# ScalarE's fp16 copy of each gated FFN row tile moves behind the next tile's tanh or conv read-out

## What is computed

```python
xn  = layernorm(x)
x   = x + (xn + mamba2(xn)) + ffn(xn)
# ffn: 512 -> 2048 -> 512
hidden = silu(xn @ W1.T) * (xn @ W3.T)
out    = fwht(hidden) @ W2.T
# mamba2: one projection to z (1024), xBC (1280), dt (16); a causal conv of 4 taps and silu on xBC;
# a state-space scan over chunks; y * silu(z); RMS norm; w_out (1024 -> 512)
```

## Time and profile before

| | |
|---|---|
| median of three runs | 968.58 us |
| the profiled execution | 965.39 us |
| its span, first to last instruction | 963.6 us |
| mean granted TensorE clock | 0.996 of full |
| busy: PE, DVE, ACT, POOL | 934.7 (97%), 555.8 (58%), 391.4 (41%), 276.1 (29%) us |
| chain that ended last, by engine | PE 67%, DVE 1%, DMA 1%, ACT 1% |
| ACT's copies, line 978 | 64, 40.2 us; before them ACT was idle for 141.3 us, waiting for DVE's line 1265 |
| POOL's `hid_lo`, line 1443 | 64, 71.2 us |

### The profile page before, as it was taken

How to read it: one execution, slowest core, us unless ns; L and a number is a source line. 1 busy time by engine, 2 the same in 40 slices (tenths; PEclk the granted TensorE clock), 3 DMA queues, 4 the chain that set the end, 5 groups by cost and what they waited for, 6 DMA issues and landing times.

```text
span 963.6 us, 13435 instructions
## 1 busy us (share of the span) xinstructions
PE 934.7 (97%) x5000; PEld 469.3 (49%) x5000; DVE 555.8 (58%) x955; ACT 391.4 (41%) x690; POOL 276.1 (29%) x354
## 2 busy tenths in 40 slices
PE   9899987989899999999999999999999999999998
PEld 4444443545344445555454445555445445555543
DVE  7876588875534756556532766566451666575421
ACT  6678874533323445233221434233222444343200
POOL 0000446352000116466110106565210104654410
PEclk9999999999999999999999999999999999999999
DMA  9798355434224335525223435436223435256123
GB/s 336 247 349 295 112 192 193 131 124 137 96 74 147 125 111 159 155 72 176 88 67 113 143 99 164 145 97 175 78 76 101 143 107 160 65 151 153 45 77 98
DMA packets 76208, 134.26 MB, mean 139 GB/s; under 512 B 7536, under 2 KB 20464, under 8 KB 74096
## 3 DMA queue, kind: packets, MB, share of 16 engines
q1 hardware_dynamic: 56640, 104.88, 34.1%
q10 hardware_dynamic: 19504, 28.53, 10.0%
HBM read 107.43 MB, written 25.95 MB: 138 GB/s over the span
## 4 chain that ended last, share of the span: by engine, by line
PE 67%; DVE 1%; DMA 1%; ACT 1%; issue 0%; DVEq 0%; ACTq 0%
PE ps L600 46%; PE ps L834 14%; PE ps L796 2%; PE ps L782 1%; PE ps L788 1%; PE ps L768 1%; DMA arena<-cs_rows 1%; PE ps L619 0%; PE ps L638 0%; PE ps L751 0%; PE ps L771 0%; DVE arena L1348 0%; DVE arena L1426 0%; ACT arena L1059 0%; DVE arena L1265 0%
## 5 line engine op out<-in xcount | busy, mean ns | idle before, releaser
L600 PE MATMUL ps<-xh,arena 128*128 128x512 f16 x1592 | 487.9, 379 | 3.4 <-DVE arena L1194 3.3
L600 PE MATMUL ps<-xl,arena 128*128 128x512 f16 x796 | 302.0, 379 | 0.0
L600 PEld LDWEIGHTS ps<-xh,arena 128*128 128x128 f16 x1592 | 158.3, 99 | 190.3 <-issue 5.9
L834 PE MATMUL ps<-arena 128*128 128x512 f16 x768 | 171.1, 379 | 0.0
L1443 POOL TENSOR_TENSOR arena<-arena 128x512 f16<-128x512 f32 x64 | 71.2, 1113 | 334.6 <-ACT arena L978 334.6
L1244 DVE SCALAR_TENSOR_TENSOR arena<-ps,cw,arena 128x511 f32<-128x511 f32 (+2 forms) x120 | 89.4, 747 | 66.9 <-ACT arena L968 65.0
L600 PEld LDWEIGHTS ps<-xl,arena 128*128 128x128 f16 x796 | 77.9, 98 | 88.7 <-issue 3.3
L834 PEld LDWEIGHTS ps<-arena 128*128 128x128 f16 x768 | 74.1, 98 | 91.2 <-issue 5.5
L978 ACT ACTIVATE arena<-arena 128x512 f16<-128x512 f32 x64 | 40.2, 629 | 141.3 <-DVE arena L1265 141.3
L1260 DVE SCALAR_TENSOR_TENSOR arena<-arena,ps 128x512 f32<-128x512 f32 x64 | 44.0, 687 | 77.3 <-ACT arena L973 77.0
L600 PE MATMUL ps<-wo_hi,arena 128*128 128x512 f16 x256 | 79.9, 384 | 3.6 <-DVE wo_lo L1333 3.4
(11 more groups left out here) (179 smaller groups left out, 1092.8 us busy)
## 6 DMA issues: line engine op xcount, KB each, us to landing
arena<-w_parts SPq DMA_DIRECT2D x198, 256.0 KB, 2.6
w_parts<-arena SPq DMA_DIRECT2D x66, 256.0 KB, 2.6
arena<-cs_rows ACTq DMA_DIRECT2D x16, 1024.0 KB, 5.7
arena<-w SPq DMA_DIRECT2D x24, 512.0 KB, 4.9
arena<-ecs_rows ACTq DMA_DIRECT2D x24, 256.0 KB, 6.9
arena<-x ACTq DMA_DIRECT2D x18, 256.0 KB, 3.4
w_mid<-arena SPq DMA_DIRECT2D x8, 512.0 KB, 3.5
arena<-w_mid SPq DMA_DIRECT2D x16, 256.0 KB, 2.6
```

Of the source, the lines that this page charges most:

```text
L600: ins = nc.tensor.matmul(out_ap, lhs(i, a), rhs(i, c), start=(i == 0 and s == 0), stop=(i == n - 1 and s == 2))
L834: ins = nc.tensor.matmul(bank(t), hw[a][:, i, t * P:(t + 1) * P], w2s[i % W2R][:, d, :], start=(i == 0 and s == 0), stop=(i == JF - 1 and ...
```

## The change

ACT's copy to `hid_hi` leaves the entry of its own U tile and is issued at the next projection tile of the stream, behind that tile's own ACT instruction: the tanh for an A or Z tile, the conv read-out (line 968) for a C tile. The 16th U tile of a batch has no next tile and keeps its copy in place. The wait that the copy needs (DVE's eviction of the U tile) and, for i = 0, the wait for the last G step of the batch before, go with it. Next tiles are A tiles but for two places in batches 1 to 3: C5 follows U0, and Z7 follows U1. No other engine's code changes. Since the list puts other entries between a U tile and the next tile, the copy now also stands behind ACT's part of those. 

```diff
+                def hidden_hi(key):
+                    i = key[1]
+                    if i == 0:
+                        act.wait_ge(w2_used.sem, w2_used.at(b, -1))
+                    act.wait_ge(evac.sem, evicted(b, key))
+                    nc.scalar.activation(hid_hi[:, i, :], hs[i % 2], ACT.Copy).then_inc(hid_h.sem, 1)
+
                 def finish(key):
...
                         nc.scalar.activation(slot, src, ACT.Tanh, scale=...).then_inc(tanh_ok.sem, 1)
-                    else:
-                        if i == 0:
-                            act.wait_ge(w2_used.sem, w2_used.at(b, -1))
-                        act.wait_ge(evac.sem, evicted(b, key))
-                        nc.scalar.activation(hid_hi[:, i, :], hs[i % 2], ACT.Copy).then_inc(hid_h.sem, 1)
+                    if p > 0 and STREAMS[b][p - 1][0] == "U":
+                        hidden_hi(STREAMS[b][p - 1])
                     if p > 0 and STREAMS[b][p - 1][0] == "C":
...
                         finish((kind, i))
+                        if POS[b][kind, i] == NT - 1:
+                            hidden_hi((kind, i))
```

## The result

The changed kernel takes 984.56 us in the median of 4 runs (984.15 to 985.51) beside 968.04 of the kernel before (4 runs, 964.78 to 969.43): a ratio of 1.0177 with the interval 1.0150 to 1.0204, slower by 16.5 us. The forecast was 974.2 with a range up to 980.0. The direction was right, the size was three times the +5.6 that I had worked out. The two profiled executions lie 20.1 us apart (985.51 and 965.39; spans 983.7 and 963.6), because the one of before was at the low end of its runs and the one of the changed kernel the highest of its four.

A forecast was written before the change was run, and what follows sets the result against it. PE bounds batches 1 to 3, with no idle time; in batch 0 PE also waits for late ACT and DVE. Batches 1 to 3 +6.6 and batch 0 -1 give +5.6 on 968.58: 974.2 us, range 967.5 to 980.0.

The forecast's parts named there:

- The slack of 1.6 us at S0: Batches 1 to 3: before the change, `Xdec` ended 1.6 us ahead of PE's start of S0.
- DVE first at the port: Batches 1 to 3, chunk 0: when `XD` ends, DVE's waiting mask product runs before `Xdec`, leaving PE idle 2.2 us at S0.
- The term was +6.6: Batches 1 to 3: PE idles 2.2 us ahead of S0 in each batch, 3 x 2.2 = +6.6 us.
- the size taken for the clock: Batches 1 to 3: PE's clock stays at 1.00 behind each S0 wait, adding nothing; bound 1.7 us more each.
- Other copies that move far ... I take 0: Copies of U5 and U9 move far, but POOL work behind them has 1 us or more slack: 0, bound +0.5 a batch.
- I let the ceiling of 13.2 go in full: Batch 0: four PE waits (9.8 us) and the clock behind two of them vanish entirely, -13.2 us.
- S0 was forecast with 5.5: Batch 0: S0 starts 4.4 to 6.6 us late behind U1's moved copy, taken as 5.5, plus 1.7 for the clock.
- S1 was forecast with 3: Batch 0: S1 starts about 3 us late behind U5's moved copy, plus 1.7 for the clock.
- One sign: Batch 0: waits at QS4 and W0 staying as before would mean a plain loss and a time above 980.
- POOL keeps its turn: Batches 1 to 3: `Xdec` runs right behind `XD` although DVE waits; +1.4 there, total 969.0 us; chance 0.10.
- Batch 0 pays for all: Batch 0 gains 9 us from the freed tanh, outweighing the +6.6 of later batches: 966.2 us; chance 0.10.
- The clock drops behind each S0: Batches 1 to 3: PE's clock falls behind each S0 wait, 3 x 1.7 = 5.1 us more: 979.3 us; chance 0.12.

The follow-up runs named there:

- pick_more: Kernel before with copies of U2, U3, U4 and U7 moved in batch 0, and all but U1's in batches 1 to 3: 960.70 us, ratio 0.9918.
- only_u11: Kernel before with only the copy of U11 of batch 0 moved: 970.56 us, ratio 1.0024.
- u11_home: Changed kernel, but the copy of U11 of batch 0 stays in its old place: 980.56 us, ratio 1.0131.
- b0_keep: Kernel before with copies moved in batch 0 only, all but those of U1, U5 and U11: 967.94 us, ratio 1.0005.
- keep9: Kernel before with copies moved in batch 0 only, all but those of U1, U5, U9 and U11: 962.76 us, ratio 0.9943.
- lo_first_late: Changed kernel, but in batch 0 DVE does an A tile's last weight split ahead of that tile's eviction: 981.94 us, ratio 1.0148.
- dec_first: Changed kernel, but in batches 1 to 3 POOL does `Xdec` of chunk 0 ahead of `XD`: 975.81 us, ratio 1.0075.
- pick: Kernel before with only the copies of U2, U3, U4 and U7 of batch 0 moved: 962.74 us, ratio 0.9948.
- later_only: Kernel before with copies moved in batches 1 to 3 only, batch 0 as before: 975.21 us, ratio 1.0083.

## Why the prediction was right in direction and wrong in size

**Batches 1 to 3: the mechanism right, the clock wrong.** The slack of 1.6 us at S0, DVE first at the port, no gain where PE has no gap, and 0 for the other copies: all stood (`Xdec` 3.95 us, PE 1.99 idle, pick_more). The term was +6.6 and the waits came to 6.0. What failed is the size taken for the clock, nothing for each wait. I gave 0.12 to a rival in which it falls behind S0, and argued against it from one stretch in which 2.0 us of idle had left it at 1.00. In the changed kernel it fell behind two of three such waits, and cost 1.4 and 1.7 more in them (3.6 and 3.9 against 2.2). This made 9.6 of 6.6.

**Batch 0, the step "Other copies that move far ... I take 0".** This is the step that failed worst: it took 0, with a bound of 0.5 a batch. I followed U5's and U9's copies by the distance they move and did not follow U11's, which passes ACT's part of E3, a place where ACT is idle for 9.86 us behind DVE. The rule that I had for S0 (what stands ahead of the copy's new place, and what stands behind `hid_lo` on POOL) was not applied to it. Of the 5.9 us of added wait at N2 it carries 3.6, and the clock behind the wait comes on top; only_u11 shows 3.1 us for it alone, u11_home 4.0 in the change. U9's, which I had followed and priced at 0, is worth 5.2 us between b0_keep and keep9. If the two add up, which no run shows, 9.2 us of batch 0 were lost at a term of 0.

**Batch 0, the contention.** In batches 1 to 3 I priced the meeting with DVE's mask product. In batch 0 I had "two short weight splits" of DVE in the sum for S0 as time that POOL waits, but not the other side: that a split itself can become twice as long (1.60 us for 0.75), all through the batch. DVE's 13.2 us more (133.24 to 146.44) lie mostly there. Y1 waits 4.0 instead of 2.1. That this comes from the splits is likely and not shown apart: it falls to 0.84 in lo_first_late, where they are shorter, but PE waits 2.0 at S1 ahead of it there. So the step "I let the ceiling of 13.2 go in full" failed too: of its 9.8 us of waits 7.1 went (1.3, 3.4 and 2.4 of 3.0), but Y1 rose by 1.9, and the clock fell at new places instead of the two old ones, as told below.

**Batch 0, S0 and S1.** S0 was forecast with 5.5 and measured 4.3. S1 was forecast with 3 and measured 0.5. The chain of my sum was nearly right, 7.0 us from the tanh of A6 (140.21) to S1 (147.23) instead of 7.6. But I took PE's step at its old distance of 4.9 from that tanh, and PE was ready only after about 6.5: behind waits of 0.6 at line 739 and 1.3 at line 810 the granted clock was 0.55 from 140 to 142 us and 0.60 from 142 to 144, where it was 1.00 before, and the matmuls ahead of S1 took 1.7 us longer.

**Batch 0, the clock.** I gave it 1.7 for each of S0 and S1 and took back 3.4 for two waits, so zero in all. Measured is 6.1 us of busy time, more than the added idle of 4.4. Behind each of the three long waits the matmuls are stretched: S0's to 3.75 us from 1.96, Y1's to 3.68 from 1.97 in the kernel before, and behind N2 the clock is at 0.53. That ahead of S1 is the fourth place.

The account: +10.5 instead of -1, and +9.6 instead of +6.6, makes 20.1 instead of 5.6 between the profiled executions. Two slips of the working do not change this: with batch 0 at +4 the sum is 979.2 and not the 978 given as the upper end of the forecast's own range, and the plain sum of POOL's instructions makes S0 3.5 us late, 4.4 only with one split of DVE. One sign did not separate what it should: the time came out above 980 although the waits at WOS and W0 were gone and QS4 had 0.6 left.

**The rivals.** "POOL keeps its turn" fell (3.95 us in all three batches, dec_first). "Batch 0 pays for all" fell for this change, but its mechanism is true of a part of it: pick gains 4.8 us. "The clock drops behind each S0" was half true. What is open is why it fell behind some waits of 1.99 us and not behind others: behind the same three waits it fell twice in the changed kernel, twice in later_only, once in u11_home and twice in lo_first_late (batches 2 and 3, 2 and 3, 2, and 1 and 3); and in pick_more it stayed at 1.00 behind waits of 2.1 to 2.3 us. No run separates the causes. Also not separated is how the rest of the loss in batch 0 divides between U9's copy and the others that start a leapfrog.

The sharing itself is as the Trainium skill has it ("SBUF — State Buffer", section "Who interferes with whom": a VectorE instruction with two SBUF inputs contends with a GpSimd instruction that reads SBUF, and the one issued first holds the shared ports for its whole instruction). This case agrees: the split of 106.06 ends at 107.66, so its own 0.75 began at 106.91, 0.2 ahead of the recorded end of `hid_lo`, and it stood still for 0.85 us because `hid_lo` had led by 0.03.

## What to carry to other kernels

When an instruction is moved in one engine's queue, write down for every single copy of it what blocking wait it now stands behind, and what stands behind its consumer on the next engine; the one that passes a wait on another engine is the dear one, and it need not be the one that moves past the most work. A move can also change which instructions of two engines start together, and make both longer without adding any: look for pairs released by the same producer. And move it per instance: here 46 moved copies gain 0.8%, by the four of batch 0 among them as far as the traces show, and 60 lose 1.8%.

## What was not expected of the hardware

- A start 0.03 us later costs an instruction nearly what the other one lasts (0.85 us beside 1.09), and it spreads: from 106.03 us on, POOL's three and DVE's three instructions take 1.09, 2.34, 2.34 and 1.60, 1.78, 3.98 us, where alone they take 1.09, 1.90, 1.90 and 0.75, 0.75, 2.29.
- In the two kinds of meeting looked at, when the holder ends and the other engine waits, the other goes next even if the holder's engine has its next instruction ready (`XD` and then the mask product at 373.58; `Xdec` at 109.38 ahead of the mask product issued at 109.89). Both cases fit "who waits longest"; for the second place the forecast had left the order open.
- The same idle of 1.99 us left the clock at 1.00 in one batch and was followed by 0.50 in two others.
- More idle can go with less time: pick_more has 16.4 us of PE's idle from 90 us to its last eight matmuls of batch 0, pick 13.6 (206.33 less 192.72 busy), and their stretches are equally long, because the clock stayed at 1.00 in the first and averaged 0.98 in the other.
